# An attention block on one core: TensorE's order where a narrow tile follows a wide one, and a last step weighed by pairs of heads

## What is computed

```
scores = einsum('bhqd,bhkd->bhqk', q, k) * SCALE      # causal
attn = softmax(scores);  y = einsum('bhqk,bhkd->bhqd', attn, v)
out = x + y.reshape(B, T, 2048) @ Wo + x_q @ w_rram.T
```

## Time and profile before

| What | Value |
|---|---|
| median of three runs | 1766.99 us |
| profiled execution, its own time | 1764.6 us |
| its span (first to last instruction) | 1762.8 us |
| PE busy | 1693.3 us, 96% of the span |
| DVE busy | 1334.8 us, 76% |
| ACT busy | 1134.8 us, 64% |
| POOL busy | 583.7 us, 33% |
| DMA queue of SP and its like (q1), share of 16 engines | 74.6% |
| mean granted TensorE clock | 0.989 of full |

### The profile page before, as it was taken

How to read it: one execution, slowest core, us unless ns; L and a number is a source line. 1 busy time by engine, 2 the same in 40 slices (tenths; PEclk the granted TensorE clock), 3 DMA queues, 4 the chain that set the end, 5 groups by cost and what they waited for, 6 DMA issues and landing times.

```text
span 1762.8 us, 29331 instructions
## 1 busy us (share of the span) xinstructions
PE 1693.3 (96%) x9200; PEld 853.3 (48%) x9200; DVE 1334.8 (76%) x3369; ACT 1134.8 (64%) x2463; POOL 583.7 (33%) x1042
## 2 busy tenths in 40 slices
PE   3689999999999999999999999999999999999998
PEld 3445545444554545545454455554454444554443
DVE  5678787768788787787878687876878867777764
ACT  5666766657566666666667566666757656666653
POOL 1223333333333233433333333333333333343320
PEclk9899999999999999999999999999999999999999
DMA  9337877878968877886879978786887888897785
GB/s 262 85 63 142 152 137 148 148 134 154 157 118 151 160 145 149 155 158 117 157 127 162 168 135 150 142 148 123 154 156 142 154 141 144 144 158 141 143 153 111
DMA packets 911877, 255.05 MB, mean 145 GB/s; under 512 B 897384, under 2 KB 899946, under 8 KB 911338
## 3 DMA queue, kind: packets, MB, share of 16 engines
q1 hardware_dynamic: 902336, 235.29, 74.6%
q10 hardware_dynamic: 8938, 15.80, 3.2%
q0 software_dynamic: 448, 2.10, 0.6%
HBM read 20.32 MB, written 8.39 MB: 16 GB/s over the span
## 4 chain that ended last, share of the span: by engine, by line
PE 77%; issue 6%; DVE 6%; ACT 4%; DMA 4%; POOL 2%; SPq 1%; ACTq 0%; DVEq 0%; POOLq 0%
PE bank L586 6%; PE bank L588 6%; PE bank L587 6%; PE bank L589 6%; PE bank L618 6%; PE bank L620 5%; PE bank L619 5%; PE bank L636 5%; PE bank L638 5%; PE bank L637 5%; PE bank L598 3%; DVE F L1312 2%; ACT P L898 2%; DMA FT<-F 2%; PE bank L591 2%
## 5 line engine op out<-in xcount | busy, mean ns | idle before, releaser
L898 ACT ACTIVATE P<-P,nm 128x512 f32<-128x512 f32 (+7 forms) x512 | 395.0, 772 | 446.7 <-DVE nm L1298 444.5
L1298 DVE CUSTOM_DVE_ANT_0 P<-bank,mask,neg 128x512 f32<-128x512 f32 (+7 forms) x512 | 402.6, 815 | 271.9 <-PE bank L598 167.3
L1510 POOL TENSOR_SCALAR sn<-sm 128x1 f32<-128x1 f32 x512 | 207.7, 406 | 932.6 <-ACT P L898 922.1
L893 ACT ACTIVATE F<-P,rc 128x512 f16<-128x512 f32 (+7 forms) x512 | 384.8, 767 | 107.9 <-DVE rc L1306 87.5
L1312 DVE SCALAR_TENSOR_TENSOR F<-P,rc,F 128x512 f16<-128x512 f32 (+7 forms) x512 | 413.7, 820 | 2.8 <-ACT F L893 2.4
L588 PE MATMUL bank<-K,Q 128*128 128x512 f16 (+3 forms) x760 | 248.5, 327 | 0.0
L586 PE MATMUL bank<-K,Q 128*128 128x512 f16 (+3 forms) x760 | 248.5, 327 | 0.0
L589 PE MATMUL bank<-K,Q 128*128 128x512 f16 (+3 forms) x760 | 248.5, 327 | 0.0
L587 PE MATMUL bank<-K,Q 128*128 128x512 f16 (+3 forms) x760 | 248.5, 327 | 0.0
L618 PE MATMUL bank<-FT,V 128*128 128x512 f16 x568 | 217.0, 382 | 14.3 <-DMA FT<-F 10.9
L619 PE MATMUL bank<-FT,V 128*128 128x512 f16 x568 | 216.0, 380 | 0.0
(11 more groups left out here) (210 smaller groups left out, 2665.4 us busy)
## 6 DMA issues: line engine op xcount, KB each, us to landing
out<-X ACTq DMA_DIRECT2D x31, 256.0 KB, 3.6
X<-in_x ACTq DMA_DIRECT2D x28, 256.0 KB, 3.2
FT<-F SPq DMA_TRANSPOSE x348, 4.2
wo<-in_Wo SPq DMA_DIRECT2D x4, 1024.0 KB, 8.6
V<-CC SPq DMA_DIRECT2D x32, 64.0 KB, 2.7
Q<-QS SPq DMA_TRANSPOSE x128, 4.0
X<-in_x SPq DMA_DIRECT2D x4, 256.0 KB, 7.5
ua<-in_Wq_up SPq DMA_DIRECT2D x1, 1024.0 KB, 11.1
```

The source lines that it names most:

```text
L893: return e.eng.activation(dst, src, ACT.Copy, scale=scale)
L898: e.eng.activation(m.P[:, u % 4, 0:w], m.P[:, u % 4, 0:w], ACT.Exp, bias=m.nm[:, u % 8:u % 8 + 1], scale=-1.0, accum_out=m.sm[:, u % 8:u % ...
L1298: e.eng.tensor_tensor_reduce(out=m.P[:, u % 4, 0:w], in0=m.pS[u % 2][:, off:off + w], in1=m.mask[:, 1024 - w:1024], scale=m.neg[:, :], sca ...
```

## The change

A step is called late where it is the last of a wide tile and the next tile is narrow (and it isn't step 127). These are steps 23, 31, 39, 55, 63, 71, 87, 95 and 103, nine in all.

- In a late step TensorE does `up_pe(n + 4)` and `combine(n - 1, 0)` between the first pair of scores and the first `weigh`. Before, `up_pe` stood behind the weighing of the first quarter and `combine(n - 1, 0)` behind that of the second and behind `down`.
- In a late step DVE writes YL between the two row maxima of the first pair, where before it wrote it behind both.
- The last step is weighed two heads at a time, `weigh_pair(0)` and `weigh_pair(1)`, with matmuls of 256 columns, each pair in the first half of a bank of its own. Each pair waits only for its own two heads' FTL. `weigh_pair(0)` stands behind `combine(125)`, `weigh_pair(1)` behind `combine(126)`. ACT and DVE write YH and YL of step 127 in two halves, and each half of `combine(127)` waits for its own.

```
+def late(n):
+    return early(n) and n < N - 1
...
+    def weigh_pair(p):
+        n = N - 1
+        b, i, g = where(n)
+        for z in range(GROUP_OF[4 * n + 2 * p], GROUP_OF[4 * n + 2 * p + 1] + 1):
+            e.wait_ge(s.ft_in[z % FSLOTS], 16 * (z // FSLOTS + 1))
+        e.wait_ge(s.yl, n - 1 + p)
+        ft = turned_at(m, n, 0, 1024 * (i + 1)).rearrange("p (h c q) -> p h c q", h=4, q=128)[:, 2 * p:2 * p + 2, :, :]
+        o = m.pY[(n + p) % 2][:, 0:256].rearrange("p (h q) -> p h q", h=2)
+        for j in range(i + 1):
+            V = m.V[:, key_slot(b, j), :, :]
+            e.eng.matmul(o, V[:, 0, :], ft[:, :, j, :], start=(j == 0), stop=False)
+            e.eng.matmul(o, V[:, 0, :], ft[:, :, i + 1 + j, :], start=False, stop=False)
+            op = e.eng.matmul(o, V[:, 1, :], ft[:, :, j, :], start=False, stop=(j == i))
+        op.then_inc(s.pv, 1)
...
-        e.wait_ge(s.yl, n + 1)
+        e.wait_ge(s.yl, n + 1 + (p if n == N - 1 else 0))
...
+            if q == 0 and late(n):
+                queries.up_pe(n + 2 * AHEAD)
+                combine(n - 1, 0)
             for j in quarter(n, q):
                 weigh(n, j)
-            if q == 0 and n + 2 * AHEAD < N:
+            if q == 0 and n + 2 * AHEAD < N and not late(n):
                 queries.up_pe(n + 2 * AHEAD)
...
-            if q % 2 and n and n + AHEAD < N:
+            if q % 2 and n and n + AHEAD < N and not (q == 1 and late(n)):
                 combine(n - 1, q // 2)
-    for n in (N - 3, N - 2, N - 1):
-        combine(n, 0)
-        combine(n, 1)
-        if n == N - 3:
-            for j in range(where(N - 1)[1] + 1):
-                weigh(N - 1, j)
+    combine(N - 3, 0)
+    combine(N - 3, 1)
+    weigh_pair(0)
+    combine(N - 2, 0)
+    combine(N - 2, 1)
+    weigh_pair(1)
+    combine(N - 1, 0)
+    combine(N - 1, 1)
...
+    def last_values_hi(p):
+        e.wait_ge(s.pv, JBASE[N - 1] + 1 + p)
+        e.wait_ge(s.c, N - 2)
+        copy(m.YH[:, (N - 1) % 2, 256 * p:256 * p + 256], m.pY[(N - 1 + p) % 2][:, 0:256], 2.0 ** -4).then_inc(s.yh, 1)
...
             if u < 4 * N:
                 maximum(u)
+                if p == 0 and late(n):
+                    values_lo(n - 1)
                 maximum(u + 1)
...
-    values_lo(N - 1)
+    last_values_lo(0)
+    last_values_lo(1)
```

More of the change, by code:

```diff
@@ L978, in scalar_attention @@
                 scaled_hi(u + 1)
-            if p and n + AHEAD >= N - 1:
+            if n == N - 1:
+                last_values_hi(p)
+            elif p and n + AHEAD >= N - 1:
                 values_hi(n)
@@ L1319, in values_lo, with last_values_lo @@
                                    op0=ALU.mult, op1=ALU.subtract).then_inc(s.yl, 1)
+    def last_values_lo(p):
+        e.wait_ge(s.yh, N + p)
+        half = slice(256 * p, 256 * p + 256)
+        e.eng.scalar_tensor_tensor(out=m.YL[:, (N - 1) % 2, half], in0=m.pY[(N - 1 + p) % 2][:, 0:256], scalar=2.0 ** -4,
+                                   in1=m.YH[:, (N - 1) % 2, half], op0=ALU.mult, op1=ALU.subtract).then_inc(s.yl, 1)
     def accumulate(t):
@@ L1376, in vector_attention @@
                 maximum(u)
+                if p == 0 and late(n):
+                    values_lo(n - 1)
                 maximum(u + 1)
-            if p == 0 and n and not first and not joined(n - 1):
+            if p == 0 and n and not first and not late(n) and not joined(n - 1):
                 values_lo(n - 1)
```

## The result

The changed kernel takes 1749.87 us, the median of four runs (1748.17 to 1750.85), against 1766.92 us for the kernel before (four runs, 1764.34 to 1771.26): 17.05 us less, a ratio of 0.990 with a 95% interval of 0.9879 to 0.9921. That is faster, as forecast, but by more than the forecast 13.2 us, and 0.6 us under the range's lower end.

A forecast was written before the change was run, and what follows sets the result against it. TensorE, busy 96% of the span, was taken as the bound. Late steps (12.2 - 2.8 - 0.8 + 1.6 - 1.0 = 9.2 us) plus end 4.0 gave 13.2 us off 1766.99: 1753.8 us, range 1750.5 to 1760.0.

The forecast's parts named there:

- The waits, and what covers them: Late steps: 1.84 us of moved work covers TensorE's FT waits, leaving 2.8 us of new standing time for YL.
- the waits are worth 12.2 us: Late steps: TensorE's eight waits for FT, listed as 10.9 us, cost 12.2 us from slot to slot.
- clock in step 23 ... 1.6 us: Behind step 23's wait: half of a half-clock stretch of little over 3 us is lost; winning it back gains 1.6 us.
- The median shown is 2.4 us above that execution ... 1766.99 - 13.2: Whole kernel: the gain from the profiled execution of 1764.6 us was subtracted from the median, giving 1753.8 us.
- `down` and XT: Late steps: `down` is reached earlier and waits 1.0 us for XT in step 23; cost 0.8 us over all.
- Given back: 1.0 us: Steps after late ones: earlier TensorE waits for the next FT, 0.6 us in step 24, 0.2 each in 56 and 88.
- The end: Last step: weighing in pairs removes 2.40 us of wait and 1.7 of half clock, less 0.1; gain 4.0 us.
- The rule on half width: Last weighings: the skill's spacing rule would make half width hardly cheaper, about 98 ns each, and the sum 1.6 us smaller.
- The rival in which weight loads show: Last weighings: loads stop hiding at half width, costing 4.7 us; gain 8.5, time 1758.5 us; chance 0.05.
- The other rivals: YL later, 1758.3 us, chance 0.08; gain given back, 1763 us, chance 0.10; YL bounds TensorE, 1777 us, chance 0.03.

The follow-up runs named there:

- e9: Changed kernel, but in late steps only `up_pe` goes ahead of the weighing and the combine stays in its old place; 1758.98 us.
- e5: Changed kernel, but in late steps DVE writes YL behind both maxima, as before; 1754.59 us.
- e12: Changed kernel, but in late steps both halves of the combine stand ahead of the weighing; 1752.36 us.
- e1: The kernel before, unchanged, run again as its own control; 1768.93 us, ratio 0.9998.
- e4: Only the end changed (last step weighed in two pairs), late steps as in the kernel before; 1767.71 us, ratio 0.9987 against the kernel before.
- e8: The kernel before, with ACT's load of x issued half a step later; 1765.04 us, ratio 0.9981 against the kernel before.
- e3: Only the late steps changed, the end as in the kernel before; 1753.08 us, ratio 0.9914 against the kernel before.
- e6: Changed kernel, but the last step is weighed whole, behind the combining of 126; 1752.68 us.
- e7: Changed kernel, but in late steps the twelve matmuls of `down` stand behind the second pair of scores; 1751.01 us.

## Why the prediction was right and where it was wrong

- **The waits, and what covers them: right against its trace.** 12.2 us of waits became 0.49, 0.26 and 0.13 us of standing ahead of the moved combine, by kind of late step (reckoned 0.50, 0.30, 0.12). e9, e5 and e12 show that each piece is placed where it counts.
- **The failed step: "the waits are worth 12.2 us" and "clock in step 23 ... 1.6 us".** These were the waits and the half clock of one execution, taken for those of every one. In three further traces with the old late steps (e1, e4, and e8, whose load of x is moved) the waits were 15.4 to 17.3 us from slot to slot, and two or three stretches of half clock stood there instead of one; the late steps took 1113.3 to 1117.0 us instead of 1108.9. The old order passes on every late landing in full, and the clock on top. The new order has 1.84 us of work in its place. Its late steps took 1099.3 to 1101.7 us in five traces: three of the change, and e3 and e6, which differ from it only at the end and in which 2.0 and 1.0 us of an FT wait came through. The mean of the four old traces is 1113.9, of the five new ones 1100.3: 13.6 us in place of 9.2. With 3.7 to 4.0 us for the end that makes 17.3 to 17.6, where the three comparisons gave 17.05, 19.7 and 15.5.
- **"The median shown is 2.4 us above that execution ... 1766.99 - 13.2".** This step saw the difference and carried it over unchanged. It was a hint that the execution lay on the fast side, so that more could be gained from a usual one: of 69 later executions of the kernel before (e1's and those beside the experiments) only eight were faster than its 1764.6 us. Their median is 1767.3 us, that of the change's 15 is 1750.2. The bounds had the same fault: for the clock they went from 3.3 us less to a tenth more, never to a second or third stretch. So the range was too narrow at its fast end.
- **The start.** It gave 3.4 us between the first two traces. Across fourteen traces the 9th `up` comes at 148.5 to 152.7 us, and both ends are met by either kind: e8, the old program but for one load, at 148.49, e7, a changed one, at 152.69. The three traces of the change alone spread from 148.84 to 152.09. So the difference is chance of the execution and not part of the gain: the four traces with the old late steps have a mean start of 150.9 us, the ten others 150.3. It moves single traces; what makes it differ wasn't tried.
- **`down` and XT: right in kind, too small.** XT waits were 0.77, 0.83, 0.51 and 0.73 us from slot to slot in steps 23, 55, 63 and 87, 2.8 us in all; before, 0.97 stood there. The net cost was 1.9 us instead of 0.8, and step 63 was not foreseen.
- **"Given back: 1.0 us": wrong, a misread row.** The weighing at 385.82 in the earlier trace rows is the last quarter of step 23. Step 24 weighs first at 388.32, so the slack was 4.4 us. In the changed trace FT of step 24 lands at 376.6 + 5.1 = 381.7 and is wanted at 382.19. No wait for FT came in step 24. The two errors cancel, 1.1 too little for XT and 1.0 too much here, so it is luck that the 9.2 us of the late steps met that trace's 9.25 so closely.

In the trace of after, the issue on SP's queue and step 24's first weighing, then the transpose's landing time; and in the trace of before, step 24's first weighing:

```profile
376.58 1.57 SPq L1687 DMA_TRANSPOSE FT<-F  x1
...
382.19 0.38 PE L623 MATMUL bank<-FT,V 128*128 128x512 f16 x1
```

```profile
DMA to landing us min/median/max: 5.1/5.1/5.1
```

```profile
388.32 0.38 PE L618 MATMUL bank<-FT,V 128*128 128x512 f16 x1
```

- **The end: right where the half clock comes.** The gain is 4.0 us in every trace that has the pairs against one with the half clock (60.5 to 60.7 without the pairs). e8's old end without it took 58.98, which prices the clock alone at 1.6 to 1.7. Over the four traces with the old end the mean is 60.2, a gain of 3.7. YL of the second pair is written in 0.42 us instead of 0.69 and done at 1740.73 + 0.42 = 1741.15, and the combine of the first pair runs until 1740.12 + 1.29 = 1741.41, so no wait shows.
- **The rule on half width: the measurement decides.** The trace has 0.109 us at 256 columns and 0.215 at 512. The Trainium skill's page (TensorE: Matmul & The Clock Gate, Back-to-back issue gap) gives 131 ns at 512 for a stream of weight loads and matmuls, which this stream doesn't follow; nor does it follow the 98 ns at 256 columns that the prediction estimated from that page. The rival in which weight loads show is out.
- **The other rivals are out.** No YL wait in a late step exceeded 0.5 us, and the gain wasn't given back: the stretch from the 112th to the 128th `up` is 233.2 us in all.

## What to carry to other kernels

In this kernel the same wait for a DMA differed from one execution to the next, and so did what the clock did behind it. Read such a wait in more than one trace, take the median's distance from the profiled run as a sign of which side that run is on, and let the range go to more waits as well as to fewer. Cutting the trace at instructions that both kernels have, and comparing stretch by stretch, separates the change's gain from the chance of the start. Work put ahead of a late transfer must come from where it isn't itself a cover: one half of the combine ahead gained, both halves gave part of it back.

## What the runs showed of the hardware

- The same transposes of the same program land at different times in different executions. The wait in step 23 was 2.3, 2.3, 4.2 and 2.8 us from slot to slot in four traces of the old order. The last FT transpose before step 23 took 4.7 to 5.3 us from issue to landing in eleven of the fourteen traces and 6.4 to 6.6 in e3, e4 and e12, and those three had the FT waits there that stand out (2.0, 4.2 and 0.6 us, each for its order). The trace of after and that of e3, the same program up to the end:

```profile
DMA to landing us min/median/max: 4.7/4.7/4.7
```

```profile
DMA to landing us min/median/max: 6.6/6.6/6.6
```

  The load of x nearby isn't needed for it: with the load moved (e8) that transpose took 5.3 us. What makes it late stays open.
- Half clock doesn't follow every pause of the same length. In the old order's traces it came behind waits of 2.32, 2.33, 2.34, 2.35, 2.50, 2.63, 2.79, 2.82 and 4.24 us in late steps, but not behind others of 2.63 and 2.91 us in e1, nor behind the 2.51 us before the last step in e8. None followed a wait under 2.3 us in any trace (the longest of these was 2.24, in e7). By the matmuls' spacing, the half clock behind the 4.2 us wait in e4 cost 2.7 us, the others 1.6 to 1.7 each. The first weighing behind that wait:

```profile
375.98 0.59 PE L623 MATMUL bank<-FT,V 128*128 128x512 f16 x1 [4.07 <-DMA FT<-F]
```

- A late landing that nothing covers shows in the scatter too: 15 runs of the full change lie between 1747.8 and 1752.6 us, where 69 of the kernel before lie between 1762.1 and 1777.8. The clock goes with it: the 23 of these with a mean granted clock of 0.987 or less took 1768.9 us or more, the 29 with 0.989 or more took 1765.3 on average.
